# The MLP's read of twelve tiles: from transposes and matrix products on TensorE to products and sums on VectorE

## The reference, cut to what matters

```python
def rat_read(res, W, gamma, beta, num_outputs):
    x = res.reshape(b, l, H, C)                     # H = 512, C = 4
    y = jnp.einsum('blhc,hoc->bloh', x, W)          # four products and their sum
    mu, var = y.mean(-1, keepdims=True), y.var(-1, keepdims=True)
    yn = (y - mu) * jax.lax.rsqrt(var + EPS)
    return (yn * gamma + beta).reshape(b, l, num_outputs * H)

qkv_in = rat_read(hidden_states, attn_read_w, attn_read_g, attn_read_b, 3)
attn_out = attention(qkv_in, qkv_w, position_ids)
hidden_states = rat_write(hidden_states, attn_out, ...)
mlp_in = rat_read(hidden_states, mlp_read_w, mlp_read_g, mlp_read_b, 2)
g_in, u_in = (mlp_in[..., :H], mlp_in[..., H:])
mlp_out = jax.nn.silu(g_in @ mlp_in_w[0].T) * (u_in @ mlp_in_w[1].T)
hidden_states = rat_write(hidden_states, mlp_out, ...)
```

## Time and profile before

| | us |
|---|---|
| three runs, median (lowest to highest) | 1636.47 (1634.73 to 1637.02) |
| profiled execution: span, first to last instruction | 1627.3 |
| median of the runs less that span | 9.2 |
| TensorE, VectorE, ScalarE, GpSimd busy in the span | 1531.8, 1129.6, 921.9, 364.1 |
| mean granted clock of TensorE | 0.983 |

### The profile page before, as it was taken

One profiled execution on the slowest core, in us unless ns is written; L12 is line 12 of the kernel. 1 busy time (PEld: TensorE's weight loads), 2 busy tenths in 40 slices (PEclk: granted clock), 3 DMA queues, 4 the chain that ended last, 5 costly groups with the idle time before them and its releaser, 6 DMA issues.

```text
span 1627.3 us, 25328 instructions
## 1 busy us (share of the span) xinstructions
PE 1531.8 (94%) x9574; PEld 1169.6 (72%) x9574; DVE 1129.6 (69%) x1782; ACT 921.9 (57%) x1702; POOL 364.1 (22%) x346
## 2 busy tenths in 40 slices
PE   7999999999999988899999999899999999999986
PEld 6567666666666656778798778798877898875554
DVE  7777745888888878644463785974776955636777
ACT  5444345888888776455543656643657644552443
POOL 1645555555433420110002000012000011001000
PEclk8999999999999999899999999999999999999998
DMA  9667677999987945356577766667766667756542
GB/s 371 204 254 243 223 181 229 276 293 284 273 233 197 253 138 189 130 185 223 202 218 233 258 226 221 214 218 232 265 233 221 223 197 237 218 180 213 203 178 104
DMA packets 127609, 360.94 MB, mean 222 GB/s; under 512 B 15744, under 2 KB 45056, under 8 KB 111872
## 3 DMA queue, kind: packets, MB, share of 16 engines
q1 hardware_dynamic: 127200, 359.19, 68.7%
q10 hardware_dynamic: 288, 0.13, 0.0%
HBM read 273.15 MB, written 86.11 MB: 221 GB/s over the span
## 4 chain that ended last, share of the span: by engine, by line
PE 74%; DVE 12%; ACT 6%; DMA 3%; issue 3%; POOL 1%; SPq 0%; DVEq 0%; ACTq 0%; POOLq 0%
PE ps L1921 21%; PE ps L1933 9%; PE ps L693 5%; PE ps L1249 5%; PE ps L1236 4%; PE ps L1272 4%; PE ps L1946 4%; PE ps L1879 3%; PE ps L1864 3%; PE ps L1809 3%; ACT a_p L1378 3%; PE ps L1824 3%; PE ps L1891 3%; DMA p_x<-in_x 2%; PE ps L652 2%
## 5 line engine op out<-in xcount | busy, mean ns | idle before, releaser
L1921 PE MATMUL ps<-m_y_split,m_win 128*128 128x512 f32 x1536 | 372.7, 396 | 2.7 <-issue 2.7
L1921 PEld LDWEIGHTS ps<-m_y_split,m_win 128*128 128x128 f32 x1536 | 284.2, 189 | 63.9 <-issue 7.1
L1308 DVE TENSOR_REDUCE a_negmax<-ps 128x1 f32<-128x640 f32 (+7 forms) x176 | 180.7, 1027 | 61.1 <-PE ps L1239 60.3
L1378 ACT ACTIVATE a_p<-ps,a_negmax 128x128 f32<-128x128 f32 (+7 forms) x256 | 188.5, 750 | 36.0 <-DVE a_negmax L1308 33.8
L1933 PE MATMUL ps<-m_wods,m_y_split 128*128 128x316 f32 x768 | 178.7, 322 | 3.8 <-DVE m_hT L2145 3.4
L2183 ACT ACTIVATE m_turned<-ps 128x512 f32<-128x512 f32 x128 | 75.0, 596 | 160.3 <-PE ps L1809 129.1
L1249 PE MATMUL ps<-ident,a_p 128*128 128x128 f32 x1152 | 157.8, 275 | 2.9 <-DVE a_pT L1321 2.0
L1236 PE MATMUL ps<-a_k,a_q 128*128 128x512 f32 (+3 forms) x384 | 124.4, 403 | 16.7 <-ACT a_p L1378 15.0
L1933 PEld LDWEIGHTS ps<-m_wods,m_y_split 128*128 128x128 f32 x768 | 128.5, 192 | 8.0 <-DVE m_hT L2145 3.7
L1249 PEld LDWEIGHTS ps<-ident,a_p 128*128 128x128 f32 x1152 | 123.5, 141 | 5.4 <-DVE a_pT L1321 3.5
L2341 POOL TENSOR_TENSOR m_scale<-m_scale,mhalf 128x2 f32<-128x2 f32 x16 | 13.0, 813 | 493.5 <-DVE m_scale L2081 493.5
(11 more groups left out here) (250 smaller groups left out, 3095.3 us busy)
## 6 DMA issues: line engine op xcount, KB each, us to landing
m_win<-mlp_in_split SPq DMA_DIRECT2D x128, 512.0 KB, 4.4
m_wods<-mlp_out_split SPq DMA_DIRECT2D x96, 316.0 KB, 3.3
p_xT<-in_xT SPq DMA_DIRECT2D x16, 1024.0 KB, 9.9
p_x<-in_x SPq DMA_DIRECT2D x16, 1024.0 KB, 10.6
a_q<-qk_split SPq DMA_DIRECT2D x64, 256.0 KB, 7.0
a_k<-qk_split SPq DMA_DIRECT2D x128, 128.0 KB, 7.2
mlp_in_split<-a_w_two SPq DMA_DIRECT2D x32, 512.0 KB, 5.5
m_hs<-in_x SPq DMA_DIRECT2D x15, 1024.0 KB, 5.6
```

The lines of the kernel that those rows point to most:

```text
L1308: V.tensor_reduce(negmax[:, n % 4, 0:len(units[n][3])], by_head(n, score_banks(n)), AX_X, ALU.max, negate=True).then_inc(max_ready, 1)
L1378: m = S.activation(dst[:, j, :], src[:, j, :], ACT.Exp, bias=negmax[:, n % 4, j:j + 1], accum_out=rsum[:, si % 2, q * 4 + hh:q * 4 + hh + 1])
L1921: m = nc.tensor.matmul(bank_of("m", blk, step), win[s][:, wl, ic, :], y[k], start=(ic == 0 and p3 == 0), stop=(ic == HCH - 1 and p3 == 2))
```

## The change: products and sums on VectorE from tile 4 on

Tiles 0 to 3 are read as before. From tile 4 on, for each quarter q, one instruction multiplies the 512 columns with both outputs' weights, which lie repeated in all partitions (`m_read_wide`, four tables of 128 x 1024), into the free buffer `m_A`, and a second sums each four neighbours into `m_y`. Statistics are then taken from `m_y` in SBUF, 512 elements at a time, and ScalarE normalises in place with two instructions. The transposes, ScalarE's copies and the read's products of these 12 tiles go. Three of the four tables are loaded in the attention phase; the fourth takes the place of `m_read` and is loaded just before tile 4, behind a wait for tile 3's last read. The load of the next "a" tile waits for the fourth sum in place of the fourth transpose.

```diff
+        def load_wide(q):
+            move(wide2[q][:, :, :], read2_rows[q].unsqueeze(0).broadcast_to([P, RD2, BLK])).then_inc(wide_loaded, 16)
...
+        def folds_of(i):
+            return 4 * (i - TB + 1) if i >= TB else 0
...
             if step == "outer":
                 dve.wait_ge(dve_own.sem, own_at[what, i])
+                if lane_before[what, i] and lane_before[what, i][0] == "a":
+                    dve.wait_ge(folded, folds_of(lane_before[what, i][1]))
...
-            if part == "stats":
+            if part == "fold":
+                c = i % TB
+                dve.wait_ge(hs_ready, nth("sum", what, i))
+                dve.wait_ge(wide_loaded, 64)
+                dve.wait_ge(turn2_mm, 8 * (i // TB))
+                dve.wait_ge(folded, folds_of(i) - 4 + q)
+                x4 = hs[hs_of[what, i]][:, BLK * q:BLK * q + BLK].unsqueeze(1).broadcast_to([P, RD2, BLK])
+                prod = Ab[0][:, 0:RD2 * BLK]
+                n = dve_own.then_inc(V.tensor_tensor(prod.rearrange("p (o f) -> p o f", o=RD2), x4, wide2[q][:, :, :],
+                                                     ALU.mult))
+                dve.wait_ge(dve_own.sem, n)
+                V.tensor_reduce(y2[c][:, :, P * q:P * q + P], prod.rearrange("p (o h c) -> p o h c", o=RD2, c=C), AX_X,
+                                ALU.add).then_inc(folded, 1)
+            if part == "stats" and i >= TB:
+                c = i % TB
+                dve.wait_ge(folded, folds_of(i))
+                for o in range(RD2):
+                    n = dve_own.then_inc(V.bn_stats(m_st[:, c, o, 0, :], y2[c][:, o, :]))
...
             if part == "norm":
                 c = i % TB
                 act.wait_ge(yscale2_ready, i + 1)
-                act.wait_ge(turn2_mm, 8 * (i // TB))
+                if i >= TB:
+                    for o in range(RD2):
+                        m = S.activation(y2[c][:, o, :], y2[c][:, o, :], ACT.Identity, bias=m_sc[:, c, 2, o:o + 1],
+                                         scale=m_sc[:, c, 1, o:o + 1])
+                    m.then_inc(y2_ready, 1)
+                    return
...
             if part == "load":
+                if (what, i) == ("a", TB):
+                    for q2 in (2, 3):
+                        wait_for_quarter(sp, "a", TB - 1, q2)
+                    load_wide(0)
...
-                        sp.wait_ge(turnq_mm, quarter["a", j, 3] + 1)
+                        if j < TB:
+                            sp.wait_ge(turnq_mm, quarter["a", j, 3] + 1)
+                        else:
+                            sp.wait_ge(folded, folds_of(j))
```

The table of places is replaced as a whole, with the four turns and four reads of "A" giving way to four folds. Two of its lines, for "A":

```diff
-       'turn2': 15.72,
-       'read2': 17.94,
+                 'fold2': 16.39,
```

More of the change, by code:

```diff
@@ L418, in program @@
         place[0] = ring_end
+        read2_place = place[0]
         read2 = sb("m_read2", [P, DCH, RD2, HPC])
+        read2_end = place[0]
         gam2 = sb("m_gamma2", [P, RD2 * HCH])
@@ L445, in program @@
         m_sc = sb("m_scale", [P, TB, 3, RD2])
+        wide2 = []
+        after, place[0] = place[0], read2_place
+        wide2.append(sb("m_read2_wide0", [P, RD2, BLK]))
+        assert place[0] == read2_end
+        place[0] = after
+        wide2 += [sb(f"m_read2_wide{q}", [P, RD2, BLK]) for q in (1, 2, 3)]
         place[0] = keep
@@ L2411, in write_sp @@
                 move(m_x[x_at][:, :], x[i]).then_inc(mx_loaded[x_at], 16)
-            if part == "turn" and q == 0:
+            if part in ("turn", "fold") and q == 0:
                 sp.wait_ge(hs_ready, nth("sum", what, i))
```

312 lines of the change are left out of this document (162 added, 150 removed).

## The result

| | us |
|---|---|
| before, median of four runs in the same comparison | 1635.60 (1631.00 to 1637.02) |
| changed kernel, median of four runs | 1621.91 (1621.67 to 1624.28) |
| ratio with its 95% interval | 0.9929, 0.9913 to 0.9944 |
| ratio of the two medians above | 0.9916 |
| forecast | 1612, range 1588 to 1645 |

What follows compares the result with a forecast made beforehand. TensorE was taken to bound the kernel, with VectorE becoming as long in blocks 1 and 2. The terms sum to -24.6 us on the span of 1627.3, giving 1602.7; with 9.2 us for the median, 1612, range 1588 to 1645.

Steps and rivals of the forecast that it cites:

- before block 0: Ahead of the MLP phase's first 512-row block: tiles 0 to 3 are read as they were, 0 us.
- block 0: First 512-row block of the MLP phase, TensorE's all through: 20 us less, 4 given back, -16 us.
- block 1, head and rest: Second 512-row block: up to its first product with the up half -3 us; after it, VectorE 93% busy, -5.3 us.
- block 2, head and rest: Third 512-row block: up to its first product with the up half -2 us; after it, VectorE 93% busy, +6.7 us.
- block 3: Last 512-row block, without a read: new places take TensorE work out of its first part, -5 us.
- median above the span: Whole kernel: the median of the runs lies 9.2 us above the profiled span.
- (b): Blocks 1 and 2 after their heads: VectorE's queue becomes the bound and isn't dense; slower, +20 us, 1656; chance 0.16.
- (c): VectorE's sums of four cost 2.45 us instead of 1.225: 42 us more, 1654; chance 0.07.
- (a): TensorE stays the bound, VectorE's work fits between: -60 us, 1576, or 1596 with 97% density; chance 0.18.
- (d): A draw: VectorE's density near 87% in blocks 1 and 2 after their heads, 1637 us; chance 0.09.

Runs made afterwards that it cites:

- e1: Changed kernel with the places of tiles 0 to 3 and the start of tile 4 as before the change: 1615.26 us, ratio 0.9885.
- e2: Kernel before with only the places of tiles 0 to 3 of the changed kernel: 1643.94 us, ratio 1.0053.
- e17: Changed kernel with one number changed, tile 1's last read at 2.905 in place of 3.36, ahead of the expert sums: 1615.81 us, ratio 0.9882.
- e18: Kernel before with one number changed, tile 1's last read at 3.36 in place of 2.8, behind the expert sums: 1642.82 us, ratio 1.0045.
- e13: Changed kernel with 74 in place of 40 idle transposes ahead of tile 2's turns, filling TensorE's wait: 1618.31 us, ratio 0.9897.
- e3: Changed kernel with a copy of 256 elements in place of each product and sum, so tiles 4 to 15 aren't read: 1592.97 us, ratio 0.9763.
- e10: e1 with the eight turns of block 3 at their old, earlier places: 1614.70 us, ratio 0.9893.
- e7: Changed kernel with all places of the kernel before, products and sums standing where the transposes stood: 1649.21 us, ratio 1.0092.
- e4: Changed kernel with only tiles 4 to 7 read on VectorE, tiles 8 to 15 on TensorE, and all places of before: 1616.51 us, ratio 0.9903.
- e8: e1 with the products of tiles 4 to 15 on GpSimd in pieces of 512, only the sums on VectorE: 1631.47 us, ratio 0.9982.
- e11: e1 with the second write and expert part of tiles 12 to 15 at their old places: 1621.67 us, ratio 0.9920.
- e6: Kernel before with the new places for the second write and expert part of tiles 8 to 11 only: 1642.37 us, ratio 1.0053.
- e15: e1 with 32 idle transposes in TensorE's wait ahead of block 0's first turn: 1615.85 us, ratio 0.9877.
- e5: Changed kernel with old places for tiles 0 to 3, and tiles 12 to 15 read on TensorE with block 2's old places: 1621.99 us, ratio 0.9917.
- e9: Changed kernel with one number put back, the load of tile 3's rows at 0.1 in place of 3.04: 1620.52 us, ratio 0.9923.

## Why the prediction fell short

By its own steps, on the profiled spans:

| step | forecast | measured |
|---|---|---|
| before block 0 | 0 | +12.1: places +8.3, later end of attention +3.8 |
| block 0 | -16 | -14.7 |
| block 1, head and rest | -3, -5.3 | -0.2, -4.6 |
| block 2, head and rest | -2, +6.7 | -5.9, +11.5 |
| block 3 | -5 | -6.4 |
| median above the span | 9.2 | 2.8 |

**The step that failed** is "Before block 0 tiles 0 to 3 are read as they were: 0", a term put at nothing; it measured 7 to 10 us. The operations were as they were, their places weren't: the table of places was replaced as a whole, and the step priced the two transfers and a wait there, but not the order. One read that was moved makes VectorE wait 6.25 us in front of work that TensorE needs, and behind the 3.91 us that TensorE then waits its granted clock is down to a half. e1 and e2 show the cost, e17 and e18 that one number makes 6 us of it, e13 that the clock's share is some 3 of the 8.3. Without it the kernel takes 1615 to 1616 us, 3 to 4 above the forecast.

**The rule was named at another place.** The forecast weighed the clock's fall after a pause (the Trainium skill, "TensorE: Matmul & The Clock Gate", section "HAM oscillation — how this bites in real kernels") for the eight tiles of blocks 1 and 2, where it priced 3.8 + 2 us each. In part this came: in these blocks TensorE's waits for VectorE grew from 6.5 to 21.5 us, and each of its eight waits of 1.8 to 7.1 us, for whatever engine, is followed by 4 us at a granted clock of 0.50 to 0.59; before there were two waits over 1.8 us and one such fall. The longest wait for VectorE, and the slice behind it:

```profile
1165.78 1.12 PE L1829 MATMUL ps<-ident,m_hs 128*128 128x128 f32 x4 [3.94 <-DVE m_hs L2090]
```

```profile
1165.78:1169.78 4.00, 2.94 (x17) 2.17 (x18) 3.87 (x11) 3.74 (x6) 0.70 (x1) 0.50 1.00 413
```

The forecast gave waits that grow to tens of us, with such clocks, as the sign of (b); it shows here in a weak form. What these falls cost isn't shown, since VectorE sets the pace there (e3). The pause that the forecast didn't look for is the one of 3.91 us at the start, where the clock's fall cost more than the 2 us of the earlier trace rows: 3.8 by the trace, of which e13's fill gave 2.9 back.

**The constant.** The median was taken as span plus 9.2 us. The changed kernel's profiled execution took 1621.67 us at a span of 1619.1, so 2.6 us lie around a span; in the experiments' executions of the kernel before it is 2.2 (1634.14 at a span of 1631.9). So the trace of before, span 1627.3, is of an execution of some 1629.5 us (an estimate from these), 7 us quicker than the median, and attention ended earlier in it than in any other trace, at 624.84. It made the forecast 6.4 us too high, the start 8.3 and attention's end 3.8 too low, the blocks 4.3: 12.1 + 4.3 - 6.4 = 10.0, the 9.9 of the miss but for rounding.

**What held.** Prices were 1.222 us for the product and 1.220 for the sum, forecast 1.22 and 1.225, and (c) is out. Block 0 is TensorE's: e3 shows that VectorE's work costs it nothing. In the rests of blocks 1 and 2 VectorE is the bound, at 91.4% and 90.0% where 93% was taken. With the forecast's work of 175.8 and 178.9 us that makes the rests 3.3 and 6.4 us longer, and since the work came out at 173.4 and 177.5, 2.6 and 1.6 shorter. Block 1's head lost 0.2 us in place of 3. The terms of block 2 and block 3 are not two findings: by e10 the later turns shift some 9 us from one to the other, and together the forecast's -0.3 stands against -0.9.

**The rivals.** (a) needed VectorE's work to fit between; e3, without that work, takes 1592.97 us, close to its 1596, and the 31 us in blocks 1 and 2 are what it left out. (b) is what the change would have been in the old order (e7, 1649; forecast 1656): what keeps the changed kernel above 87% is the new order. (d) had the draw at 87% density, which the rests exceed.

Nearly the whole gain is block 0's (e4). In blocks 1 to 3 together the two traces differ by 5.6 us. That block 1's -4.8 comes from its places and not from the engine isn't shown: the read on TensorE with the new places of block 1 wasn't run.

## What to carry to other kernels

Where a table of places is replaced, compare the order of every part of it, also of work that is "as before", and look for an instruction that stayed while its producer moved behind long work on the other engine: everything that stands behind the waiting instruction is late too. Moving work from a bound engine pays where the other engine has real slack; here four of twelve tiles brought nearly the whole gain, and the others made VectorE the bound. A kernel's single trace can be 8 us off its median, so a part of 4 us is read from several executions. A forecast against a median needs the profiled execution's own time, not its span and the median of other runs.

## What the runs showed of the hardware

**GpSimd and VectorE slow each other.** In e8 GpSimd's product of 512 elements took 1.616 us in the mean, while its other tensor_tensor instructions of that size take 1.27 to 1.28, and VectorE's operations of 1536 elements rose (the last row is the update that the products of its own tile wait for):

```profile
L2447 POOL TENSOR_TENSOR m_A<-m_hs,m_read_wide 128x512 f32<-128x512 f32 x72 | 114.5, 1616 | 295.7 <-DVE m_hs L2103 198.4 <-DVE m_y L2146 84.1 <-DVE m_y L2150 13.2
...
L2062 DVE TENSOR_TENSOR m_A<-m_delta,m_gate 128x1536 f32<-128x1536 f32 x30 | 58.7, 1958 | 1.0
L2093 DVE SCALAR_TENSOR_TENSOR m_A<-m_A,m_gate 128x1536 f32<-128x1536 f32 x30 | 56.0, 1868 | 0.0
L2103 DVE TENSOR_TENSOR m_hs<-m_hs,m_A 128x1536 f32<-128x1536 f32 x28 | 49.2, 1758 | 0.9
```

In the changed kernel the first two of VectorE's rows take 1.758 and 1.755 us. The means hide two kinds: of VectorE's instructions of 1536 elements on lines 2062, 2093 and 2098, the 12 that overlap a product of GpSimd took 2.70 to 2.85 us, the 84 others 1.74 to 1.89. One of them:

```profile
1247.31 2.75 DVE L2062 TENSOR_TENSOR m_A<-m_delta,m_gate 128x1536 f32<-128x1536 f32 x1
```

The sums of 1024 elements (line 2146), which read one buffer, took 1.21 us with and without a product beside them. In blocks 1 and 2 of e8 VectorE is rid of 39 us of products and its other instructions take some 43 us longer than in e1, so it is busy for 197.45 and 207.68 us there, in e1 for 197.07 and 203.00. The move gave VectorE nothing. The Trainium skill ("SBUF — State Buffer", section "SBUF: two separate sides") says that a GpSimd operation which reads SBUF and a VectorE operation with two SBUF inputs exclude each other; the 12 long and 84 short instructions agree with it.

**The clock falls in some executions of the same code and not in others.** e10 and e11 have the same start. Their gaps are 61.6 and 65.7 us, without a wait of TensorE over 2 us there in either until the turns of block 0. The stretch behind tile 2's transposes takes 26.2 us in e10 and 31.6 in e11. In e11 the granted clock is 0.57 at 652.17 to 656.17, behind a slice with 2.20 us of matmuls, and 0.70, 0.50 and 0.52 from 668.17 to 680.17:

```profile
648.17:652.17 4.00, 2.20 (x21) 1.96 (x19) 3.05 (x9) 3.80 (x9) 0.73 (x1) 1.00 1.02 382
652.17:656.17 4.00, 4.00 (x25) 4.00 (x24) 3.86 (x8) 2.38 (x6) 0.00 (x0) 0.57 1.01 428
```

The gaps of the eight other traces with these start places and fills are 61.1 to 61.6 (before, e1, e6, e15), 63.4 (e7) and 65.6 to 65.7 (e4, e5, e8); with the changed start they are 69.9, 70.7 and 70.8 (changed kernel, e2, e9), but 66.2 in e3. So a single trace tells such a part only to 4 us, and the medians decide.
